# Reordering the start of both halves of a gated MLP stage: store order, adapter factors and a separate buffer for gated rows

## The chip, the cores and the metric

One core of a Trainium2 chip runs the whole program. The metric is the device time in microseconds of one execution; the median of several runs counts. All matrix products are in float32: each operand is split into a rounded part and a remainder, and every product is three matmuls (high x high, high x low, low x high).

## What is computed

Two residual layers on x of 8 x 256 x 1024. The first is a linear layer whose weight is quantised group by group with a codebook of 8 levels and carries a low-rank delta. The second is a gated MLP (gate, up, down, hidden width 2752) with rank-16 adapters picked for each batch row.

```python
# first layer, 1024 x 1024
lora_delta = lora_B @ lora_A * (32.0 / 64)
wg = (weight + lora_delta).reshape(O, I // 128, 128) / scale
w_q = (cb[searchsorted(thresholds, wg)] - wg + wg) * scale
x = x + x @ (w_q + lora_delta).T
# second layer, F = 2752
def lora_add(base, inp, A, B):
    Ab, Bb = A[0][itok], B[0][itok]          # (8, 16, in), (8, out, 16)
    t = einsum('bri,bni->bnr', Ab, inp)
    return base + einsum('bor,bnr->bno', Bb, t) * 0.5
gate = lora_add(x @ W_gate.T, x, A_gate, B_gate)
up   = lora_add(x @ W_up.T,   x, A_up,   B_up)
act  = silu(gate) * up
x = x + lora_add(act @ W_down.T, act, A_down, B_down)
```

## The kernel before

Every engine has its own program, written out by hand, with its order fixed and semaphores between the engines. An engine that waits holds up all that stands behind it in its program; SyncE (SP) and ScalarE (ACT) also issue the DMAs, in program order.

Stage 1, the first layer, ends at about 230 us. x (2048 tokens) is kept in four column blocks c of 512 tokens. `main(i)` on TensorE is one block of 128 output rows times 512 tokens, 24 matmuls, 5.4 us. There are 32; the last six are 26 and 27 (output block 7, c 0 and 1, called LAST0 and LAST1), 28 and 29 (blocks 6 and 7, c = 2), 30 and 31 (c = 3). Two PSUM banks take turns: `main(i)` waits until `out_x1(i - 2)` on ScalarE has copied the bank to a staging buffer (L1980: `pe.wait_ge(s_x1t, i - 1)`); SyncE then stores it with `store_x1(i)` to `XR_d`.

Stage 2, the gate and up products, runs from 230 to about 1173 us. It is a two-level blocked scheme with seven products in place of eight (Strassen's, in the form with few sums). The work is cut into tiles `it` of the hidden width, 11 for each half h of the tokens (it 0 to 10 and 11 to 21), for each tile m = 0 (gate) and m = 1 (up), and for each of these seven products p. The row is mm = 2 it + m, the product number u = 7 mm + p; a product is 12 matmuls, 2.7 us. Tile 0 and tile 11, the first of each half, are the short ones of 96 rows, with the adapter's A rows riding along in the other 32. What each product needs:
- weights: SyncE loads W rows (`load_wn(mm)`), VectorE transposes four blocks L11, L21, L22, L12 (`w_tr`), SyncE stores them for the second half (`store_wt(mm, n)`, n = 0 to 3, to `WT_d`), GpSimd makes the sums S1, S2 (`w_s12`), the difference that overwrites L21 (`w_s3`, L852) and the one that overwrites L12 (`w_s4`, L860). `w_s3(mm)` waits for the store of L21 in the first half: `gp.wait_ge(s_wst[1], 16 * (mm + 1))`. ScalarE rounds the block of product u to `rh` (`hi(u)`, L994), VectorE makes the remainder `rl` (`lo(u)`, L1335). `hi(3)` takes the block that `w_s3(0)` made.
- tokens: once for each half, seven token operands. SyncE loads them to `xr` (`load_raw`, L535; `load_x` in the second half), in the first half VectorE makes four sums (`x_sum`, L1415), ScalarE rounds (`x_hi(h, q)`, L1007), VectorE takes the remainder (`x_lo(h, q)`, L1344). Product q of the first row waits for `x_lo(h, q)`.
- PSUM is emptied by `take(mm, p)` on VectorE (L1360 to L1378) and the copy of bank 1 to `tm` on ScalarE.
- gate and up adapters: the rows of B for a tile are loaded by `load_bn` (ACT), transposed by `b_tr` (VectorE), subtracted by `b_sub`, rounded by `b_hi` (ACT), their remainder made by `b_lo`, and spread by `store_bs(it, g)` (SyncE, six small DMAs, L532) to `bs`. The factors of the tokens are `ts`: `ts_hi` (ACT, L1070) and `ts_lo` (VectorE, L1427), made in the first tile of each half out of `take(row, 2)` and `take(row, 4)`. TensorE first uses them in `ride_lora(h, 0)` before product 8 of the half (L1864).
- the gated rows: `silu` and `gated(it, n)` (L1445) leave four blocks in `ev[:, 1]`. They are stored raw (`store_raw`, ACT), summed by GpSimd (`act_sum(it, 0..3)`, L868 to L879) and stored (`store_s`, SyncE), and multiplied by the down adapter's A on TensorE (`td(n)`, L1893 and L1894) with its own rounding and remainder (`a_hi`, `a_lo`, L1421; `ad` from the transposed rows `ar`, which share the buffer `tm`). `take` of the next up row waits until all this is done.
- W_down is transposed into `dt_` on VectorE and combined on GpSimd in four rounds between rows 13 and 20, the others from row 29 on.

Stage 3, from 1173 us on, multiplies the stored products with W_down.

Of the kernel before, what the change touches and what calls it, by code (L numbers as in the profile page):

```python
# [23 lines left out]
def cond_resid_kernel(  # L24
# [84 lines left out]
    with ctx:  # L109
# [205 lines left out]
        dt_ = aux("dt", [P, 4, CH], f32, 2)  # L315
        araw = aux("araw", [P, 4, DI], f32, 2)
# [157 lines left out]
        with nc.Block() as block:  # L474

            @block.sync
            def _(sp):
# [86 lines left out]
                def dn_load(rd, half):  # L564
                    if rd == 0 and half == 0:
                        sp.wait_ge(s_xts, 64 * XTN)
                    if rd == DN1 and half == 0:
                        sp.wait_ge(s_tdst, 16 * 4)
                    wait(sp, s_dtr, 4 * rd + 2 * half)
# [163 lines left out]
                store_wt(0, 1)  # L733
# [105 lines left out]
            def _(gp):  # L839
# [22 lines left out]
                def act_sum(it, n):  # L862
                    r = slice(0, rows_of(jof(it)))
                    a11, a12, a21, a22 = (ev[r, 1, n_, :] for n_ in range(4))
# [78 lines left out]
                for u in range(END + 7):  # L943
# [10 lines left out]
                    turn = (5, 5, 7, 7) if first(it - 1) else (4, 4, 6, 6) if it == NJ else (1, 1, 3, 4)  # L954
# [29 lines left out]
            def _(act):  # L984
# [69 lines left out]
                def a_hi(n):  # L1054
# [4 lines left out]
                    nc.scalar.copy(ah[r, :], ev[r, 1, (0, 3, 1, 2)[q], :]).then_inc(s_ah, 1)  # L1059
# [23 lines left out]
                def store_raw(it, q):  # L1083
# [3 lines left out]
                    act.dma_start(LT_d[(M1, M4, M2)[q], h, j, r, :], ev[r, 1, (0, 3, 2)[q], :]).then_inc((s_a11, s_a22, s_a21)[q], 16)  # L1087
# [146 lines left out]
                for u in range(END):  # L1234
# [15 lines left out]
                    if (mm, p) == (NM // 2 + 1, 6):  # L1250
# [858 lines left out]
```

## Time and profile before

| | us |
|---|---|
| median of 3 runs (1591.92 to 1593.32) | 1592.16 |
| the profiled execution | 1591.67 |
| its span, first to last instruction | 1590.0 |
| TensorE (PE) busy | 1566.0 (98%) |
| VectorE (DVE) busy | 1236.0 (78%) |
| ScalarE (ACT) busy | 565.9 (36%) |
| GpSimd (POOL) busy | 531.1 (33%) |
| chain that ended last: PE / DVE / issue / DMA | 88% / 6% / 2% / 1% |

TensorE is busy nearly all the time, its mean granted clock is 0.997 of full speed. The share of the span says little about the change; what matters are the few microseconds at which TensorE has nothing to do, who ends them, and what that engine did before. In the rows, "[2.33 <-ACT ts L1070]" behind an instruction is the idle time of its engine just before it and what ended it; "x4" is the number of instructions of one merged piece.

### The profile page before, as it was taken

Reading aid. Unit: us, or ns where it says so; the run is one execution under the profiler, and the core shown is the slowest. Engines: PE = TensorE matmul, PEld = TensorE weight load, DVE = VectorE, ACT = ScalarE, POOL = GpSimd, SP = SyncE. Lnnn points to the kernel's source line nnn. Section 1 sums busy time; section 2 is a strip of 40 time slices with the busy share of each in tenths; the row PEclk is TensorE's granted clock in tenths of the full one; section 3 lists DMA queues with packets and bytes.
Section 4 is the critical chain, followed back from the end, with each engine's and each line's share of the span. In section 5 each row is a group of like instructions: output and inputs, shape, how many; then the busy total and the mean of one; then the engine's idle time right before and its main releaser. Section 6 shows DMA issues by size and latency. Waiting matters only on the chain.

```text
span 1590.0 us, 21056 instructions
## 1 busy us (share of the span) xinstructions
PE 1566.0 (98%) x6936; PEld 1286.9 (81%) x6936; DVE 1236.0 (78%) x1583; ACT 565.9 (36%) x1005; POOL 531.1 (33%) x401
## 2 busy tenths in 40 slices
PE   7999999999999999998999999999999999999999
PEld 5888887888888888886888888888888888888887
DVE  8999869888888999988777887878776576795453
ACT  6311146333333333365333333333343233233231
POOL 4410022465654565625344555556410000000000
PEclk9999999999999999999999999999999999999999
DMA  9652274567777888782435666666468667676553
GB/s 303 133 111 82 68 226 104 149 204 221 222 218 191 224 234 220 232 279 70 122 119 144 185 182 183 162 182 177 141 199 222 157 174 196 160 214 204 159 184 119
DMA packets 368460, 281.25 MB, mean 177 GB/s; under 512 B 225120, under 2 KB 266848, under 8 KB 368224
## 3 DMA queue, kind: packets, MB, share of 16 engines
q1 hardware_dynamic: 246976, 240.77, 52.7%
q10 hardware_dynamic: 119296, 33.33, 9.0%
q0 software_dynamic: 2080, 5.80, 1.9%
q8 instruction: 57, 0.93, 0.2%
q14 instruction: 51, 0.42, 0.1%
HBM read 166.27 MB, written 110.85 MB: 174 GB/s over the span
## 4 chain that ended last, share of the span: by engine, by line
PE 88%; DVE 6%; issue 2%; DMA 1%; ACT 1%; ACTq 1%; SPq 0%; DVEq 0%
PE bank L1842 20%; PE bankA L1842 14%; PE bankC L1842 13%; PE bank L2077 10%; PE bankC L2077 7%; PE bankA L2077 6%; PE bankT L1990 5%; PE bank L1990 5%; PE bankT L2077 3%; DVE xl L1344 1%; PE bankT L1893 1%; PE bankT L1894 1%; PE bankC L1858 1%; DVE rl L1335 1%; DMA xr<-XR_d 1%
## 5 line engine op out<-in xcount | busy, mean ns | idle before, releaser
L994 ACT CAST rh<-wt 128x512 fp32r<-128x512 f32 x253 | 155.2, 620 | 387.8 <-PE bank L1842 92.9
L1335 DVE TENSOR_TENSOR rl<-wt,rh 128x512 fp32r<-128x512 f32 x253 | 241.9, 964 | 35.6 <-ACT rh L994 35.4
L1504 DVE TENSOR_TENSOR opl<-opl,oph 128x512 fp32r<-128x512 f32 (+1 forms) x154 | 107.8, 701 | 155.5 <-ACT oph L1131 155.4
L1842 PE MATMUL bank<-xh,rh 128*128 128x512 f32 x528 | 206.1, 390 | 1.0 <-DVE rl L1335 0.5
L1842 PE MATMUL bank<-xl,rh 128*128 128x512 f32 x528 | 205.7, 390 | 0.0
L1842 PE MATMUL bank<-xh,rl 128*128 128x512 f32 x528 | 205.6, 389 | 0.0
L1131 ACT CAST oph<-opl 128x512 fp32r<-128x512 f32 (+1 forms) x154 | 95.5, 621 | 268.7 <-DMA opl<-LT_d 263.6
L1842 PE MATMUL bankA<-xh,rh 128*128 128x512 f32 x352 | 138.5, 393 | 0.0
L1842 PE MATMUL bankA<-xl,rh 128*128 128x512 f32 x352 | 138.4, 393 | 0.0
L1842 PE MATMUL bankA<-xh,rl 128*128 128x512 f32 x352 | 138.2, 393 | 0.0
L1842 PE MATMUL bankC<-xh,rh 128*128 128x512 f32 x352 | 137.4, 390 | 0.3 <-DVE xl L1344 0.3
L1842 PE MATMUL bankC<-xh,rl 128*128 128x512 f32 x352 | 137.1, 390 | 0.0
L1842 PE MATMUL bankC<-xl,rh 128*128 128x512 f32 x352 | 137.1, 389 | 0.0
L1842 PEld LDWEIGHTS bank<-xh,rh 128*128 128x128 f32 x528 | 99.1, 188 | 23.6 <-issue 1.5
L845 POOL TENSOR_TENSOR wt<-wt 128x512 f32<-128x512 f32 x33 | 46.7, 1416 | 211.8 <-DVE wt L1329 180.2
L1842 PEld LDWEIGHTS bank<-xh,rl 128*128 128x128 f32 x528 | 99.1, 188 | 20.7
L1842 PEld LDWEIGHTS bank<-xl,rh 128*128 128x128 f32 x528 | 99.2, 188 | 20.5
L1360 DVE TENSOR_TENSOR ev<-bankA,tm 128x1024 f32<-128x1024 f32 x44 | 53.5, 1216 | 52.7 <-PE bankA L1858 48.8
L860 POOL TENSOR_TENSOR wt<-wt 128x512 f32<-128x512 f32 x33 | 49.6, 1504 | 121.5 <-DMA WT_d<-wt 85.5
L2077 PE MATMUL bank<-opl,oph 128*128 128x512 f32 (+1 forms) x231 | 90.0, 390 | 0.0
L2077 PE MATMUL bank<-oph,opl 128*128 128x512 f32 (+1 forms) x231 | 90.0, 389 | 0.0
L2077 PE MATMUL bank<-oph 128*128 128x512 f32 (+1 forms) x231 | 89.9, 389 | 0.0
(214 smaller groups left out, 3644.2 us busy)
## 6 DMA issues: line engine op xcount, KB each, us to landing
opl<-LT_d SPq DMA_DIRECT2D x148, 256.0 KB, 2.9
WT_d<-wt SPq DMA_DIRECT2D x88, 256.0 KB, 3.3
RT_d<-dt SPq DMA_DIRECT2D x70, 256.0 KB, 3.2
opl<-RT_d SPq DMA_DIRECT2D x70, 256.0 KB, 3.8
LT_d<-ev ACTq DMA_DIRECT2D x60, 256.0 KB, 2.7
wb<-WT_d SPq DMA_DIRECT2D x44, 256.0 KB, 3.4
wt<-WT_d SPq DMA_DIRECT2D x44, 256.0 KB, 3.5
dn<-in_L_cond_W_down_dram SPq DMA_DIRECT2D x86, 128.0 KB, 3.8
```

The source lines that it names most:

```text
L845: tt(wsrc(mm, S1), wsrc(mm, L21), wsrc(mm, L22), ALU.add).then_inc(s_sum, 1)
L860: tt(wsrc(mm, L12), wsrc(mm, L12), wsrc(mm, S2), ALU.subtract).then_inc(s_sum, 1)
L994: nc.scalar.copy(rh[:, v % RING, 0:KH * rows], wsrc(mm, RSRC[p])).then_inc(s_hi, 1)
L1131: nc.scalar.copy(oph[0:rows, L_AT[n % NL], :], opl[0:rows, L_AT[n % NL], :].bitcast(f32)).then_inc(s_lh, 1)
L1335: dv.tensor_tensor(rl[:, v % RING, 0:KH * rows], wsrc(mm, RSRC[p]), rh[:, v % RING, 0:KH * rows].bitcast(f32), ALU.subtract).then_inc(s_lo, 1)
L1344: dv.tensor_tensor(xl[:, s, k:k + 2, :], xr[:, s, k:k + 2, :], xh[:, s, k:k + 2, :].bitcast(f32), ALU.subtract).then_inc(s_xlo, 1)
L1360: dv.tensor_tensor(e[:, 0:2, :], bankA[r, :, :], tm[r, None, :].to_broadcast([r.stop, 2, CH]), ALU.add).then_inc(s_ev, 1)
L1504: dv.tensor_tensor(opl[0:rows, L_AT[n % NL], :], opl[0:rows, L_AT[n % NL], :].bitcast(f32), oph[0:rows, L_AT[n % NL], :].bitcast(f32), ALU ...
L1842: last = te.matmul(OUT[p], a[:, u % RING, cols], b[:, OPND[p], k, :], start=k == 0 and n == 0, stop=k == KH - 1 and n == 2 and (p in (0, 1 ...
L1858: te.matmul(OUT[p][0:rows, :], bs[:, m, t, half * rows:(half + 1) * rows], ts[:, t, m, :], start=False, stop=True).then_inc(s_pd, 1)
L1990: last = te.matmul(bankY[i % 2], a[o % 3][:, k, :], b[c][:, k, :], start=(k == 0 and n == 0), stop=(k == KD - 1 and n == 2))
L2077: last = te.matmul(out_, a[0:rows, L_AT[n % NL], tok], b[0:rows, R_AT[k], :], start=(k == 0 and i == 0), stop=(k == NJ - 1 and i == 2))
```

## The change

It has three parts.
- The start of stage 2, first half. On SyncE `store_wt(0, 1)`, which stood ahead of the token loads, goes behind the last of them, behind `store_bs(0, 0)`, `store_bs(0, 1)` and `store_wt(0, 3)`; the loads of the up weights of tile 0 (`load_wn(1)`) and the other stores are re-sorted. On ScalarE `load_bn(1)` and `b_hi(1)` come into the last part of stage 1, `out_x1` of block 6, c = 2, ahead of `load_wa(1)`, and `x_hi(0, 3)` ahead of the last `out_x1`. On VectorE `b_tr(1)`, `b_sub(1)`, `b_lo(1)` come ahead of the loop, the four `x_sum` stand together, `w_tr(1, 0)` and `w_tr(1, 1)` go behind `x_lo(0, 2)`.
- The start of the second half. The gated rows of tile 10 go to a buffer of their own, `gx`, in the place of `dt_`, and the transposed adapter rows of tile 11 to `arx`, in the place of `dn`. The waits that protected `ev` in row 23 are gone; in their stead `gated(10, 0)` waits for the W_down stores and the fifth W_down round for all users of `gx`.
- What is done with tile 10's rows moves: `act_sum(10, 0..3)` from products 4, 4, 6, 6 of tile 11 to products 12, 12 and to 2, 3 of tile 12; `a_hi` from 3, 8, 10 to 8, 11, 13, `a_lo` from 5, 9, 10 to 9, 11, 13, `td` from 3, 8, 10, 12 to 3, 10, 12 and 0 of tile 12; `ad_lo(11)`, `td_copy(0)` and `take_td(0)` to products 1 and 2 of tile 12.

```diff
@@ the buffers
+        gx = aux("gx", [P, 4, CH], f32, 2)
+        arx = aux("arx", [P, 2, 2, Q], f32, 1)
+        def gate(it, r, q):
+            return gx[r, q, :] if it == NJ - 1 else ev[r, 1, q, :]
+        def down_rows(it):
+            return arx if it == NJ else ar
@@ SyncE
                 sp.wait_ge(s_main, LAST0 + 1)
-                store_wt(0, 1)
                 load_raw(0, 0, KH, 0, s_x[0])
                 load_raw(1, 0, KH, 3, s_x[3])
...
                 load_raw(1, KH, KD - 1, 6, s_x[6])
+                store_bs(0, 0)
+                store_bs(0, 1)
                 store_wt(0, 3)
-                load_wn(1)
+                store_wt(0, 1)
+                store_x1(TURN[KD - 2, 2])
                 store_wt(0, 0)
                 store_wt(0, 2)
+                load_wn(1)
+                store_x1(TURN[KD - 1, 2])
                 store_bd(KD - 1)
-                store_x1(TURN[KD - 2, 2])
-                store_x1(TURN[KD - 1, 2])
-                store_bs(0, 0)
                 store_x1(TURN[KD - 2, 3])
                 store_x1(TURN[KD - 1, 3])
-                store_bs(0, 1)
@@ sums_at, SyncE
-                    return (6, 7, 8, 9) if first(it - 1) else (5, 6, 7, 8) if it == NJ else (1, 2, 4, 5)
+                    return (6, 7, 8, 9) if first(it - 1) else (13,) if it == NJ else (1, 2, 4, 5)
...
+                    if it == NJ + 1 and 7 * m + p in (0, 3, 4):
+                        store_s(NJ - 1, 1 + (0, 3, 4).index(7 * m + p))
@@ GpSimd
-                    turn = (5, 5, 7, 7) if first(it - 1) else (4, 4, 6, 6) if it == NJ else (1, 1, 3, 4)
+                    turn = (5, 5, 7, 7) if first(it - 1) else (12, 12, None, None) if it == NJ else (1, 1, 3, 4)
...
+                    if u == 14 * (NJ + 1) + 2:
+                        act_sum(NJ - 1, 2)
+                    if u == 14 * (NJ + 1) + 3:
+                        act_sum(NJ - 1, 3)
@@ ScalarE, ahead of the loop
                 hi(3)
                 hi(4)
+                load_bn(1)
+                x_hi(0, 0)
+                out_x1(TURN[KD - 2, 2])
                 load_wa(1)
-                x_hi(0, 0)
                 bd_copy(KD - 1)
-                out_x1(TURN[KD - 2, 2])
                 out_x1(TURN[KD - 1, 2])
+                b_hi(1)
                 x_hi(0, 1)
                 out_x1(TURN[KD - 2, 3])
                 x_hi(0, 2)
+                x_hi(0, 3)
                 out_x1(TURN[KD - 1, 3])
-                x_hi(0, 3)
@@ ScalarE, in the loop
-                    act_tail(u, (6, 8, 10) if first(it - 1) else (3, 8, 10) if it == NJ else (0, 3, 6))
+                    act_tail(u, (6, 8, 10) if first(it - 1) else (8, 11, 13) if it == NJ else (0, 3, 6))
@@ VectorE, take
-                        if m == 1:
+                        if m == 1 and it != NJ:
                             wait(dve, s_a11, 16 * it)
@@ VectorE, gated
+                    if it == NJ - 1 and n == 0:
+                        dve.wait_ge(s_ds, 4 * DN1)
+                        for sem_ in s_raw + s_dst:
+                            dve.wait_ge(sem_, 16 * DN1)
@@ VectorE, ahead of the loop
                 x_sum(0)
                 x_lo(0, 0)
+                b_tr(1)
+                b_sub(1)
                 x_sum(1)
                 x_sum(2)
+                x_sum(3)
+                b_lo(1)
+                x_lo(0, 1)
+                x_lo(0, 2)
                 w_tr(1, 0)
                 w_tr(1, 1)
-                x_lo(0, 1)
-                x_lo(0, 2)
-                x_sum(3)
@@ VectorE, in the loop
-                    dve_tail(u, (6, 8, 10) if first(it - 1) else (5, 9, 10) if it == NJ else (1, 4, 7))
+                    dve_tail(u, (6, 8, 10) if first(it - 1) else (9, 11, 13) if it == NJ else (1, 4, 7))
@@ TensorE
-                    td_at(u, (6, 8, 10, 12) if first(it - 1) else (3, 8, 10, 12) if it == NJ else (0, 3, 6, 9))
+                    td_at(u, (6, 8, 10, 12) if first(it - 1) else (3, 10, 12, None) if it == NJ else (0, 3, 6, 9))
+                    if u == 14 * (NJ + 1):
+                        td(4 * NJ - 1)
```

## Rows read from the trace of the kernel before

**Rows 1.** Busy time by stretch: PE, PEld, DVE, ACT, POOL (instructions), granted clock, DMA share, GB/s

```profile
230.00:260.00 30.00, 26.65 (x107) 20.53 (x106) 28.52 (x32) 17.51 (x28) 8.31 (x6) 0.94 0.39 103
320.00:700.00 380.00, 379.57 (x1673) 313.60 (x1672) 332.35 (x406) 138.62 (x244) 214.64 (x157) 1.00 0.81 224
...
256.66:260.07 3.41, 3.41 (x10) 2.67 (x9) 3.41 (x5) 1.47 (x4) 1.28 (x1) 0.51 0.43 115
```

**Rows 2.** Timeline of TensorE: start us, duration us, engine, line, operation, idle before

```profile
219.00 0.39 PE L1990 MATMUL bank<-lxh,lwh 128*128 128x512 f32 x1
...
256.35 0.52 PE L1864 MATMUL bankC<-ts,bs 128*96 128x512 f32 x1 [2.33 <-ACT ts L1070]
```

**Rows 3.** Timeline of TensorE at the start of the second half

```profile
722.24 0.47 PE L1893 MATMUL bankT<-ah,ad 128*128 128x512 f32 x1 [2.40 <-DVE al L1421]
...
726.68 0.71 PE L1864 MATMUL bankC<-ts,bs 128*96 128x512 f32 x1 [3.52 <-issue]
```

**Rows 4.** Timeline of ScalarE: `hi(3)`, `x_hi(0, 0)`, `out_x1(28)`; four issues of `load_an`

```profile
209.15 0.63 ACT L994 CAST rh<-wt 128x512 fp32r<-128x512 f32 x1
...
210.56 2.00 ACT L1007 CAST xh<-xr 128x1024 fp32r<-128x1024 f32 x2 [0.27 <-issue]
...
217.83 0.58 ACT L1173 COPY x1t_st<-bank 128x512 f32<-128x512 f32 x1
...
716.45 1.89 ACTq L1043 DMA_DIRECT2D an<-Ad_d  x4
```

**Rows 5.** Timeline of GpSimd: `w_s3(0)`

```profile
205.30 1.29 POOL L852 TENSOR_TENSOR wt<-wt 128x512 f32<-128x512 f32 x1
```

**Rows 6.** Line L497 from 202 to 203 us: the store of L21, issued 202.86

```profile
DMA to landing us min/median/max: 2.2/2.2/2.2
```

**Rows 7.** Timeline of SyncE's DMA issues: last token load, first and last of six `store_bs`

```profile
209.72 0.84 SPq L535 DMA_DIRECT2D xr<-XR_d  x1
...
220.18 1.21 SPq L532 DMA_DIRECT2D bs<-bh  x2
...
223.34 0.59 SPq L532 DMA_DIRECT2D bs<-bt  x1
```

**Rows 8.** Line L497 from 216.3 to 216.6 us: a store issued 216.38

```profile
DMA to landing us min/median/max: 8.4/8.4/8.4
```

**Rows 9.** Timeline of VectorE at the first start: `x_sum`, `x_lo`, `take(0, 4)`, `b_tr(1)`

```profile
214.16 2.29 DVE L1415 TENSOR_TENSOR xr<-xr 128x2048 f32<-128x2048 f32 x1 [3.06 <-DMA xr<-XR_d]
...
221.45 5.60 DVE L1415 TENSOR_TENSOR xr<-xr 128x2048 f32<-128x2048 f32 x2 [2.60 <-DMA xr<-XR_d]
...
236.17 4.63 DVE L1344 TENSOR_TENSOR xl<-xr,xh 128x1024 fp32r<-128x1024 f32 x4 [1.19 <-ACT xh L1007]
...
252.58 1.23 DVE L1372 TENSOR_TENSOR ev<-bank,ev 128x1024 f32<-128x1024 f32 x1
...
254.32 0.44 DVE L1385 STREAM_TRANSPOSE bt<-bn 128x256 f32<-128x256 f32 x1
```

**Rows 10.** Timeline of VectorE: `ts_lo` alone, at the second start, beside one GpSimd operation

```profile
273.02 0.88 DVE L1427 SCALAR_TENSOR_TENSOR ts<-ev,half_of,ts 32x256 fp32r<-32x256 f32 x2
...
716.79 2.84 DVE L1427 SCALAR_TENSOR_TENSOR ts<-ev,half_of,ts 32x256 fp32r<-32x256 f32 x2
...
721.40 0.69 DVE L1421 TENSOR_TENSOR al<-ev,ah 128x512 fp32r<-128x512 f32 x1
...
722.37 1.41 DVE L1335 TENSOR_TENSOR rl<-wt,rh 128x512 fp32r<-128x512 f32 x1
723.81 2.77 DVE L1427 SCALAR_TENSOR_TENSOR ts<-ev,half_of,ts 32x256 fp32r<-32x256 f32 x2
...
743.49 1.92 DVE L1427 SCALAR_TENSOR_TENSOR ts<-ev,half_of,ts 32x256 fp32r<-32x256 f32 x2
```

**Rows 11.** Timeline of GpSimd at the second start: `act_sum(10, 3)`, `w_s4(23)`

```profile
723.19 1.71 POOL L879 TENSOR_TENSOR s1a<-ev 128x512 f32<-128x512 f32 x1
724.86 1.44 POOL L860 TENSOR_TENSOR wt<-wt 128x512 f32<-128x512 f32 x1
```

More of the change, by code:

```diff
@@ L863, in act_sum @@
                     r = slice(0, rows_of(jof(it)))
-                    a11, a12, a21, a22 = (ev[r, 1, n_, :] for n_ in range(4))
+                    a11, a12, a21, a22 = (gate(it, r, n_) for n_ in range(4))
                     if n == 0:
@@ L1058, in a_hi @@
                     wait(act, s_tdm, n)
-                    nc.scalar.copy(ah[r, :], ev[r, 1, (0, 3, 1, 2)[q], :]).then_inc(s_ah, 1)
+                    nc.scalar.copy(ah[r, :], gate(it, r, (0, 3, 1, 2)[q])).then_inc(s_ah, 1)
                 def ts_hi(h, m, t):
@@ L1086, in store_raw, with ad_hi @@
                     act.wait_ge(s_av, 3 * it + q + 1)
-                    act.dma_start(LT_d[(M1, M4, M2)[q], h, j, r, :], ev[r, 1, (0, 3, 2)[q], :]).then_inc((s_a11, s_a22, s_a21)[q], 16)
+                    act.dma_start(LT_d[(M1, M4, M2)[q], h, j, r, :], gate(it, r, (0, 3, 2)[q])).then_inc((s_a11, s_a22, s_a21)[q], 16)
+                def ad_hi(it):
+                    act.wait_ge(s_ar, it + 1)
+                    wait(act, s_tdm, 4 * it)
+                    wait(act, s_z, 1)
+                    for t in range(2):
+                        ins = nc.scalar.copy(ad[:, :, t, t, 0, :], down_rows(it)[:, :, t, :])
+                    ins.then_inc(s_adh, 1)
                 def act_tail(u, at_):
@@ L1249, in _ @@
                         a_hi(4 * (it - 1))
[L1250 to L1261 removed]
+                    act_tail(u, (6, 8, 10) if first(it - 1) else (8, 11, 13) if it == NJ else (0, 3, 6))
+                    if (m, p) == ((1, 0) if it % NJ in (0, 1) else (0, 5)) and 0 < it < NIT - 1:
+                        b_hi(it + 1)
+                    if live and m == 1 and p == (5 if it % NJ == 1 else 4) and it != NJ:
+                        ad_hi(it)
+                    if u == 14 * (NJ + 1) + 1:
+                        ad_hi(NJ)
+                        td_copy(0)
                     if (m, p) == ((1, 1) if first(it) else (1, 6)) and it != NJ - 1 and it + 2 < NIT:
@@ L1268, in _ @@
                         wait(act, s_ev, 4 * (mm - 1) + 1)
-                        if m == 0:
+                        if m == 0 and it != NJ + 1:
                             wait(act, s_ad, it)
@@ L1284, in _ @@
                         store_raw(it, p // 2 - 1)
-                    if it < NIT and first(it) and (m, p) == (0, 2):
+                    if it == NJ and (m, p) == (0, 2):
                         load_bn(it + 1)
@@ L1362, in take @@
                     if p == 3:
-                        if m == 1:
+                        if m == 1 and it != NJ:
                             wait(dve, s_a21, 16 * it)
@@ L1368, in take @@
                     if p == 4:
-                        if m == 1:
+                        if m == 1 and it != NJ:
                             wait(dve, s_a22, 16 * it)
@@ L1473, in dn_tr @@
                     wait(dve, s_dst[(0, 1, 3, 2)[b]], 16 * rd)
+                    if rd == DN1 and b == B11:
+                        dve.wait_ge(s_as, 4 * NJ)
+                        dve.wait_ge(s_al, 4 * NJ)
+                        for sem_ in (s_a11, s_a22, s_a21):
+                            dve.wait_ge(sem_, 16 * NJ)
                     if rd == DN1:
@@ L1752, in _ @@
                             dve.wait_ge(s_an, 128 * (it + 1))
-                            dve.wait_ge(s_ev, 4 * mm + 1)
-                            dv.transpose(tm[:, 0:P],
+                            if it == NJ:
+                                dve.wait_ge(s_dtr, 4 * DN1)
+                            else:
+                                dve.wait_ge(s_ev, 4 * mm + 1)
+                            dv.transpose(down_rows(it)[:, :, :, :].rearrange("p f t r -> p (f t r)"),
                                          an[:, :, :, :].rearrange("p f t r -> p (f t r)")).then_inc(s_ar, 1)
-                        if p == 6 and it % NJ != NJ - 1:
+                        if p == 6 and it % NJ != NJ - 1 and it != NJ:
                             ad_lo(it)
+                    if u == 14 * (NJ + 1) + 2:
+                        take_td(0)
+                        ad_lo(NJ)
                     for rd in range(NJ):
@@ L1767, in _ @@
                             dn_tr(rd, B22)
-                    if mm == NM // 2 + 1 and p == 6:
-                        take_td(0)
                     if mm == NM // 2 + 4 and p in (3, 4):
```

22 lines of the change are left out of this document (7 added, 15 removed).

## The prediction

> **What bounds the kernel now.** I read the stretches of the span first, then TensorE's idle gaps, then for each gap the order of time of the engine that ends it. Between 320 and 700 us TensorE is busy 379.57 of 380 us [rows 1]: nothing that leaves its work alone can gain there. What can be won or lost lies in two places. From 230 to 260 us it is busy 26.65 of 30 us, at a mean clock of 0.94 [rows 1]. The longest wait there is for the second adapter matmul of the first row (`ride_lora(0, 0)`), which starts at 256.35 after 2.33 us of idle [rows 2]; the stretch behind it runs 3.41 us at a granted clock of 0.51 [rows 1], the 1.2 GHz level of the two, after the engine had stood still, which is another 3.41 x 0.49 = 1.7 us. The second place is the start of the second half: 2.40 us for the remainder `al` (`td(41)`) and 3.52 us before `ride_lora(1, 0)` at 726.68 [rows 3], again followed by a low clock. In both the reader is to see VectorE working without a pause: it is the engine that comes late. A third point has no gap yet: `main(30)` starts at 219.00 [rows 2] and needs the copy `out_x1(28)`, which ScalarE starts at 217.83 and takes 0.58 us over [rows 4]. That is 0.6 us of slack, and much of the change lies ahead of it.
>
> **Part 1, SyncE's order at the first boundary.** The token rows of half a layer are now asked for ahead of `store_wt(0, 1)`; that saves them one issue (about 0.4 us). What decides is where the store goes: from 202.86 to behind the last token load, behind twelve adapter stores (`store_bs(0, 0)` and `(0, 1)`) and behind `store_wt(0, 3)`. Somebody waits for it: `w_s3(0)` on GpSimd overwrites the block L21 with L11 - L21 and must first see it stored. Now it runs at 205.30 [rows 5], because the store was issued at 202.86 and landed in 2.2 us [rows 6]. Behind `w_s3(0)` stands ScalarE's `hi(3)` (it copies that block), and ScalarE and VectorE work in program order. So in turn:
> - SyncE is through with the last token load at 209.72 + 0.84 = 210.56; six adapter stores take 223.34 + 0.59 - 220.18 = 3.75 us of issue [rows 7], twelve 7.5, one weight store about 0.45: the store of L21 goes out at 218.5 instead of 202.86.
> - Its landing is not to be seen in the trace of before at that time. Bounds: 2.2 us with a quiet queue [rows 6], 8.4 us for the one at 216.38 that had a weight load and others ahead of it [rows 8]. I take 2.5, near the quiet one, since the weight load of tile 1 is now behind the store and the last token load (11.7 us for 0.75 MB while sharing the queue with it) should be done by 217. Landing 221.0, `w_s3(0)` 1.29 us [rows 5], so `hi(3)` at 222.4 instead of 209.15 [rows 4].
> - ScalarE then has `hi(4)`, the four issues of `load_bn(1)` (1.9 us, as four issues of `load_an` [rows 4]), `x_hi(0, 0)` (2.0 us) and the copy of 0.58 us [rows 4]: `out_x1(28)` ends at 222.4 + 0.1 + 1.9 + 2.0 + 0.6 = 227.0. `main(30)` starts there, not at 219.00: TensorE stands 8 us and takes about 1 us more at the low clock. The last x1 product ends at 239.1 (now 229.9) and the first gated stage's product 8 would be reached at 261.1.
> - VectorE: `lo(3)` and `lo(4)` stand behind `hi(3)`, `x_sum(0)` can start 2.0 us after it, at 224.4 instead of 214.16 [rows 9], +10.2. From there its work runs on without its two pauses of 2.60 and 1.19 us [rows 9], which are covered now, -3.8. `b_tr(1)`, `b_sub(1)`, `b_lo(1)` come in front (0.44, 0.29 and 0.38 us, the first in [rows 9]), with two hand-overs: +1.4. The two sums that took 5.60 us [rows 9] beside a GpSimd operation take 2 x 2.29, -1.0. `take(0, 4)`, now at 252.58 [rows 9], ends 6.8 us later. Without `b_tr(1)` between it and `ts_lo(0, 0, 1)` a little is won: `ride_lora(0, 0)` at 263.05 instead of 256.35, **+6.7 us**. TensorE, there at 261.1, still waits 2 us and pays its 1.7 us of low clock as before.
> So here the moved sums (`x_sum(3)` in one go) and the early factors of tile 1 do what they say, save about 3 us of pauses and 1.1 us behind the ride, and are paid for by a start 10 us late. Moved past `load_wn(1)` on SyncE are also `store_x1(28)` and two weight stores; SyncE waits for `out_x1(28)` until 227, so the weights of tile 1 are asked for at 228 to 233. `w_tr(1, 0)` needs them at about 241: hidden. The adapter stores land long before `b_tr(1)` at 229, and its rows too: hidden.
>
> **Part 2, the second half.** Four things leave VectorE's way to `ts_lo(1, 0, 1)`. The remainder `a_lo(41)` moves from ahead of it to product 9: -0.6 us (0.69 busy [rows 10]). GpSimd's four `act_sum(10, ...)` (the last of them, 1.71 us from 723.19, covers most of the second `ts_lo` [rows 11]) go to products 12 and, of the next tile, 2 and 3. `ts_lo` takes 0.88 us when GpSimd is idle, 1.92 beside one operation of it, and 2.84 and 2.77 here [rows 10]. `w_s3(23)` moves up beside the first `ts_lo` and `w_s4(23)`, at 724.86 in [rows 11] and released by `lo(163)`, beside the second, so I take 1.92 for both: -0.9 and -0.85 (bound: -1.9 each if nothing overlaps, 0 if the overlap stays). `lo(163)` drops from 1.41 [rows 10] to 0.69: -0.7. Sum **-3.1 us**: the ride at 723.6. `td(41)` is no longer in front of it and costs nothing where it is now (its two operands are made one and two products earlier). The 2.40 us wait before it does not come back on its own; it only becomes part of the wait for the ride, 719.9 to 723.6. The low clock behind is 1.7 to 2.1 us in either case.
> The Trainium skill's page "SBUF — State Buffer", section "SBUF: two separate sides", says the pair of ports that VectorE and GpSimd share is held for a whole instruction and that the loser blocks fully. By that a `ts_lo` could lose a whole GpSimd operation, some 1.3 to 1.7 us; part 2 would then be -2.3 instead of -3.1.
> The new buffer `gx` adds waits to `gated(10, 0)` for stores of W_down tiles that SyncE issues three products (8 us) earlier at the latest: nothing. `take` of row 23 no longer waits; it didn't wait long before. `td_copy(0)`, `take_td(0)` and `ad_lo(11)` go two or three products later, before `td(44)` needs them: nothing; if that cover failed, some 1.8 us of VectorE time would be late there.
>
> **Sum.** Against the profiled execution, 1591.67 us with a span of 1590.0: +6.7 - 3.1 = +3.6, so 1595.3; the median of the three runs is 0.5 above it, 1592.16, and goes to **1595.8 us**.
>
> **The rivals.**
> - The second boundary gives all back (not slower). If both `ts_lo` fall to 0.88 and the low clock goes too, part 2 is -5.2 - 1.9 = -7.1 and the time 1591.8. For it: the waits there are 5.9 us and VectorE is the only cause. Against: `w_s4(23)` is released just as the second `ts_lo` starts. Chance 0.14.
> - The late store is hidden (faster). If `w_s3(0)` were not in the way, the start would win the two pauses less the wait for the adapter stores, some -3 with the low clock -4.7, and the time would be 1584 to 1587. Against: there is no other path from the store to `hi(3)`. This is also the case that the change does what its order intends. Chance 0.08.
> - The late store is later still (slower). With the 8.4 us of [rows 8], `hi(3)` comes at 228.3 and everything behind it 5.9 later: 1601.7. It decides where the queue is still full at 218.5. Chance 0.1.
> - One of the moved steps crowds its new place (sums beside VectorE at products 12 to 14, `td(42)` at product 12 with its remainder only one product earlier): +1 to +3 on the forecast. Chance 0.08.
> The Trainium skill's page "DMA: Bandwidth & Descriptors", section "Queues, rings and completion order", says that on each DMA engine descriptors are consumed in ring order, which speaks against this change: the store of L21 would have to wait for all that was asked for ahead of it. That is the mechanism of the third rival, whose price stands above from a row.
>
> **How the numbers follow.** The forecast's own case has 0.6 and reaches from 1593 to 1598.5 (landing of 2.2 to 3.8 us, part 2 from -2.3 to -4.5). The range down to 1590.0 takes in the first rival, up to 1600.0 the fourth and the lower part of the third; left out are the hidden store and the full queue. A difference of 0.2%, 3.2 us, is about what a measurement of this kernel tells from none: 1595.4 is its edge, and the forecast lies just beyond. Of its 0.6 I put 0.36 beyond and 0.24 within; with the rivals: slower 0.36 + 0.10 + 0.07, same 0.24 + 0.14 + 0.01, faster 0.08.
>
> **What would show it.** Right: `w_s3(0)` (L852 of before) near 221, the rh casts 3 and 4 near 222.5, a TensorE gap of about 8 us in the x1 products at 219, the first `xr` sum on VectorE near 224.4, the ride at 263. In the second half, `ts_lo` of 1.8 to 2 us and one gap of 3 to 4 us instead of two. Wrong: no gap at 219, or the weight store landing by 212; then the whole first term falls. If `ts_lo` keeps 2.8 us without `act_sum` beside it, part 2 shrinks to -1.3.

## The result, and the profile after

| | before | after |
|---|---|---|
| median of 18 runs each, us | 1591.96 | 1596.34 |
| lowest to highest, us | 1587.91 to 1594.29 | 1593.06 to 1598.59 |
| profiled execution, us | 1591.67 | 1595.51 |
| its span, us | 1590.0 | 1593.9 |

The change makes the kernel slower: the ratio is 1.0025, 95% interval 1.0019 to 1.0032, or 4.4 us by the medians. The forecast was 1595.8 us, with a range of 1590 to 1600.

One thing first, for every comparison of traces below. The part of the program ahead of the change isn't equally long in each execution: the last transpose, just ahead of `main(28)`, comes 0.72 us later in after than in before, and 0.65 to 2.24 us later in ten of the eleven other traces that were taken, 0.36 us earlier in one. "Net" below means that this start is taken off.

TensorE after the change, in the same view as [rows 1]: from, to, length, busy time of PE, PEld, DVE, ACT and POOL, granted clock, DMA share, GB/s:

```profile
219.00:228.00 9.00, 1.02 (x5) 0.52 (x4) 3.87 (x3) 3.80 (x7) 2.95 (x3) 0.79 0.35 101
228.00:231.00 3.00, 3.00 (x7) 2.35 (x8) 2.97 (x4) 0.47 (x1) 0.00 (x0) 0.50 0.85 295
230.00:260.00 30.00, 30.00 (x131) 24.74 (x131) 29.66 (x29) 17.14 (x23) 6.89 (x5) 0.98 0.33 101
...
264.31:268.00 3.69, 3.69 (x16) 3.10 (x17) 3.37 (x4) 2.20 (x5) 1.30 (x1) 1.00 0.50 133
326.00:706.00 380.00, 379.61 (x1673) 313.46 (x1672) 332.42 (x406) 139.40 (x244) 214.51 (x157) 1.00 0.80 224
```

TensorE stands still from 219.9 to 227.87, where it had no gap [rows 2], and starts again at half clock, the 1.2 GHz level. The middle is untouched: 0.4 us idle in 380, as in [rows 1]. And there is a surprise in the fourth line: behind the wait for the first ride the granted clock is 1.00, where it was 0.51 in before.

The chain of the first gap, in the timelines of SyncE (the last adapter store and two weight stores, the second of which is the store of L21), GpSimd, ScalarE and VectorE of after:

```profile
218.52 0.59 SPq L542 DMA_DIRECT2D bs<-bt  x1
219.16 1.06 SPq L507 DMA_DIRECT2D WT_d<-wt  x2
```

```profile
222.18 1.26 POOL L865 TENSOR_TENSOR wt<-wt 128x512 f32<-128x512 f32 x1 [16.07 <-DMA WT_d<-wt]
223.38 0.53 POOL L955 MEMSET ad<- 128x512 f32 x1
223.87 1.26 POOL L873 TENSOR_TENSOR wt<-wt 128x512 f32<-128x512 f32 x1
```

```profile
223.48 0.62 ACT L1011 CAST rh<-wt 128x512 fp32r<-128x512 f32 x1 [13.49 <-POOL wt L865]
...
227.24 0.58 ACT L1198 COPY x1t_st<-bank 128x512 f32<-128x512 f32 x1
```

```profile
224.13 2.15 DVE L1358 TENSOR_TENSOR rl<-wt,rh 128x512 fp32r<-128x512 f32 x2 [15.77 <-ACT rh L1011]
226.20 2.28 DVE L1438 TENSOR_TENSOR xr<-xr 128x2048 f32<-128x2048 f32 x1
228.51 2.36 DVE L1367 TENSOR_TENSOR xl<-xr,xh 128x1024 fp32r<-128x1024 f32 x2
230.79 0.44 DVE L1408 STREAM_TRANSPOSE bt<-bn 128x256 f32<-128x256 f32 x1
...
263.33 0.88 DVE L1450 SCALAR_TENSOR_TENSOR ts<-ev,half_of,ts 32x256 fp32r<-32x256 f32 x2
```

The reader is to see one wait handed on three times. GpSimd stood 16.07 us for the store, ScalarE 13.49 us for GpSimd's `w_s3(0)`, VectorE 15.77 us for ScalarE's cast. TensorE, with a gap of 7.98 us, then gets `out_x1(28)`:

```profile
227.87 0.79 PE L2029 MATMUL bank<-lxh,lwh 128*128 128x512 f32 x1 [7.98 <-ACT x1t_st L1198]
...
264.31 0.44 PE L1903 MATMUL bankC<-ts,bs 128*96 128x512 f32 x1 [1.82 <-ACT ts L1087]
...
729.48 0.71 PE L1903 MATMUL bankC<-ts,bs 128*96 128x512 f32 x1 [3.34 <-issue]
...
743.71 0.47 PE L1932 MATMUL bankT<-ah,ad 128*128 128x512 f32 x1 [0.39 <-DVE al L1444]
```

The last two rows are the second half. Its two waits of 2.40 and 3.52 us [rows 3] are one of 3.34 us, and there is a new small one at `td(42)`. VectorE and GpSimd there:

```profile
722.87 1.80 DVE L1450 SCALAR_TENSOR_TENSOR ts<-ev,half_of,ts 32x256 fp32r<-32x256 f32 x2
...
726.80 0.65 DVE L1358 TENSOR_TENSOR rl<-wt,rh 128x512 fp32r<-128x512 f32 x1
727.48 1.89 DVE L1450 SCALAR_TENSOR_TENSOR ts<-ev,half_of,ts 32x256 fp32r<-32x256 f32 x2
...
742.87 0.69 DVE L1444 TENSOR_TENSOR al<-gx,ah 128x512 fp32r<-128x512 f32 x1
```

```profile
722.24 1.75 POOL L865 TENSOR_TENSOR wt<-wt 128x512 f32<-128x512 f32 x1
727.58 1.51 POOL L873 TENSOR_TENSOR wt<-wt 128x512 f32<-128x512 f32 x1 [3.60 <-DVE rl L1358]
```

The account of the 3.8 us between the two profiled executions, by how far the same instruction is shifted: start +0.72; first ride +7.96, so +7.24 for the change; +6.36 a few products behind it (-1.60, the low clock that did not come) and +6.05 through the middle; +3.61 at the last stage, so -2.44 for the second half; +3.84 at the end.

### The profile page after: what moved, and what is told of

Read it like the earlier page. It is cut to its first block, busy times and chain, and to the rows that moved or that the text cites. A ratio compares the mean times of both kernels' runs of the same rounds, so it can differ in the third digit from the quotient of the medians.

```text
span 1593.9 us, 21059 instructions
## 1 busy us (share of the span) xinstructions
PE 1565.2 (98%) x6936; PEld 1286.7 (81%) x6936; DVE 1240.1 (78%) x1583; ACT 566.3 (36%) x1005; POOL 528.7 (33%) x401
## 4 chain that ended last, share of the span: by engine, by line
PE 87%; DVE 7%; issue 3%; ACT 1%; DMA 1%; ACTq 1%; SPq 0%; POOL 0%; DVEq 0%; POOLq 0%
PE bank L1881 19%; PE bankA L1881 14%; PE bankC L1881 13%; PE bank L2118 10%; PE bankC L2118 7%; PE bankA L2118 6%; PE bank L2029 4%; PE bankT L2029 4%; PE bankT L2118 3%; DVE xl L1367 2%; PE bankT L1932 1%; PE bankT L1933 1%; PE bankC L1897 1%; DVE rl L1358 1%; PE bankA L1897 1%
## 5 line engine op out<-in xcount | busy, mean ns | idle before, releaser
L873 POOL TENSOR_TENSOR wt<-wt 128x512 f32<-128x512 f32 x33 | 47.4, 1437 | 108.7 <-DMA WT_d<-wt 71.1
```

The source lines that it names most:

```text
L873: tt(wsrc(mm, L12), wsrc(mm, L12), wsrc(mm, S2), ALU.subtract).then_inc(s_sum, 1)
```

## The experiments

Theory A, from the trace: the late store of L21 is the whole loss, and without it the first part would win what its other edits save. Rival: something else of the first part costs too. The first four runs take the change apart.

**One statement back.** The kernel after, with the store of L21 ahead of the token loads as in before:

```diff
                 sp.wait_ge(s_main, LAST0 + 1)
+                store_wt(0, 1)
                 load_raw(0, 0, KH, 0, s_x[0])
...
                 store_wt(0, 3)
-                store_wt(0, 1)
```

> The changed kernel with one line put back: the store of block L21 of tile 0 goes out ahead of the token loads again, all else stays. Theory (the late store holds up hi(3), and through it out_x1(28), main(30), x_sum(0)): no TensorE gap in the x1 products at 219, w_s3(0) back at 205 to 206, x_sum(0) near 214, ride_lora(0, 0) at 252 to 255, time 10 to 12 us below the changed kernel, 1584 to 1587. Rival 1 (the early adapter factors make a new wait of the same size: b_tr(1) on VectorE behind the twelve adapter stores): x_sum(1) starts at 222 or later, ride not before 256, time 1588 to 1591. Rival 2 (the gap at 219 comes from something else): gap stays, time 1595 or more.

Measured: 1591.27 us (11 runs), ratio to before 0.9999 (0.999 to 1.0008). 5.1 us of after come back by moving one store, and the gap at 219 is gone. But it is 1591, not 1584 to 1587: the number of rival 1, at the upper edge of its range. The timeline of VectorE in this kernel says why:

```profile
213.84 2.29 DVE L1438 TENSOR_TENSOR xr<-xr 128x2048 f32<-128x2048 f32 x1 [1.34 <-DMA xr<-XR_d]
216.16 2.36 DVE L1367 TENSOR_TENSOR xl<-xr,xh 128x1024 fp32r<-128x1024 f32 x2
225.44 0.45 DVE L1408 STREAM_TRANSPOSE bt<-bn 128x256 f32<-128x256 f32 x1 [6.92 <-DMA bs<-bt]
...
227.10 6.89 DVE L1438 TENSOR_TENSOR xr<-xr 128x2048 f32<-128x2048 f32 x3
```

`b_tr(1)` overwrites `bt` and must see the adapter stores landed. SyncE issued the last of them at 219.10, and they took up to 6.2 us to land (line L542, issues of 218.5 and 219.1):

```profile
DMA to landing us min/median/max: 4.7/5.5/6.2
```

So VectorE stands 6.92 us with three token sums behind the waiting instruction, and TensorE gets a new wait in the first gated products, with a low clock behind it (a mean of 0.64 from 236.70 to 241.00):

```profile
236.70 0.47 PE L1881 MATMUL bankA<-xh,rh 128*128 128x512 f32 x1 [2.54 <-issue]
```

In after this wait is invisible, since VectorE reaches `b_tr(1)` only at 230.79: the late store hid it.

**The first part alone**, on the kernel before (all edits of the first boundary, none of the second half; this diff stands for them):

```diff
+                store_bs(0, 0)
+                store_bs(0, 1)
                 store_wt(0, 3)
-                load_wn(1)
+                store_wt(0, 1)
...
                 x_lo(0, 0)
+                b_tr(1)
+                b_sub(1)
                 x_sum(1)
                 x_sum(2)
+                x_sum(3)
```

> The kernel before with only the first-half part (orders of SyncE, ScalarE, VectorE ahead of the loop). Theory: an 8 us gap ahead of main(30), ride_lora(0, 0) 6.5 to 7.5 us late, one low-clock stretch of 1.7 us possibly gone: 1597 to 1599. Rival (both parts are needed together, they interact): not within 1 us of the sum before + 6.5.

Measured: 1599.77 us (4 runs), ratio 1.0052 (1.0036 to 1.0068): +7.8 us, 0.8 above the upper edge of what was expected. The ride's net shift is +8.1, more than the 7.2 of after. The difference is on ScalarE, in the eight DMA issues (`load_an`) ahead of its casts: from the first to the end of the last they took 5.20 us here (two of 1.91 us together, then six of 3.26) and 3.66 us in after, and VectorE's remainders waited 0.68 us for the casts.

```profile
259.06 3.26 ACTq L1043 DMA_DIRECT2D an<-Ad_d  x6
262.42 1.14 ACT L994 CAST rh<-wt 128x512 fp32r<-128x512 f32 x2 [3.48 <-issue]
```

**SyncE's order alone.** Before, with only the list of SyncE's issues at the first boundary taken from after, and VectorE's and ScalarE's orders left alone.

> The kernel before with only SyncE's new order ahead of the loop; ScalarE and VectorE as before. Theory: the same late store, hi(3) at 222 to 223, a gap of about 8 us ahead of main(30), and as w_tr(1, 0) stands ahead of the token remainders and its weights are asked for late, 2 to 3 us more on VectorE: ride_lora(0, 0) 9 to 11 us late, 1600 to 1602. Rival (the gap needs load_bn(1) and x_hi(0, 0) ahead of out_x1(28)): gap under 3 us, time under 1596.

Measured: 1601.83 us (one run), its span 1600.2. The same chain: `w_s3(0)` at 222.42 after 16.14 us of waiting, a gap of 8.15 us. The net shift of the ride is +8.5. The highest of 15 runs of before beside it was 1593.73 us, so one run is enough to see the loss. So the order of SyncE is the loss, and the other edits of the first part win back 0.4 us of it at the ride, by one trace of each.

**The second part alone**, on the kernel before (`act_sum(10, ...)`, `a_lo(41)`, the new `gx`, the later `td` steps):

```diff
-                    turn = ... else (4, 4, 6, 6) if it == NJ else ...
+                    turn = ... else (12, 12, None, None) if it == NJ else ...
...
-                    td_at(u, ... else (3, 8, 10, 12) if it == NJ ...)
+                    td_at(u, ... else (3, 10, 12, None) if it == NJ ...)
```

> The kernel before with only the second-half part of the change (gx, arx, moved sums, a_hi, a_lo, td). Theory: the two waits of 5.9 us there become one of 3.5, of the 3.1 us won about 0.6 are lost again at td(42): 2.4 us below the kernel before, 1589 to 1590. Rival (what was won in the changed kernel at this point came from the first part's disturbance): 0 to 1 us below.

Measured: 1587.56 us (6 runs), ratio 0.9976 (0.9963 to 0.999). It beats both kernels, and is 1.4 us below the expected range. In its trace the second half wins only 1.2 us (shift -2.53 in the middle, -3.77 at the last stage), with 5.12 us at a clock of 0.50 behind the ride. The rest, 3.6 us net of the start, came ahead of it, in code that is the same in both kernels. 1.6 of that is one event: no low clock behind the first ride. The other 2.0 are shorter waits (none of 0.48 us at 238.68, one of 0.31 us and not 0.28 and 0.81 us at the down adapter's matmuls near 306 and 319) and shifts that I can't assign. That ride has the same wait as in [rows 2], 2.33 us, but the stretch behind it has a granted clock of 1.00 and not of 0.51 [rows 1]:

```profile
257.01 0.44 PE L1898 MATMUL bankC<-ts,bs 128*96 128x512 f32 x1 [2.33 <-ACT ts L1087]
```

```profile
257.50:261.00 3.50, 3.50 (x17) 2.89 (x16) 3.50 (x6) 1.92 (x4) 1.30 (x1) 1.00 0.44 114
```

By the medians the parts are +7.8 and -4.4 us, +3.4 together, and the whole change is +4.4. With intervals of about 2.5 and 2 us to either side of the parts, an interaction between them is not shown.

**The wait in store_back taken away.** Theory B: what is left in `store_back` is the 6.92 us in front of `b_tr(1)`.

```diff
                 x_lo(0, 0)
-                b_tr(1)
-                b_sub(1)
                 x_sum(1)
                 x_sum(2)
                 x_sum(3)
-                b_lo(1)
                 x_lo(0, 1)
                 x_lo(0, 2)
+                b_tr(1)
+                b_sub(1)
+                b_lo(1)
```

> This is the kernel of the run store_back (the change with the L21 store ahead of the token loads again), with the factors of tile 1 (b_tr(1), b_sub(1), b_hi(1), b_lo(1)) moved from ahead of the three later token sums to behind x_lo(0, 2). Theory: in store_back VectorE stood 6.92 us in front of b_tr(1), for the twelve adapter stores that SyncE issues behind the last token load, and all three sums stood behind it; that made the 2.54 us wait of TensorE at 236.70 and the low clock behind it. With b_tr(1) behind the sums x_sum(1) starts near 221, as in the kernel before, TensorE has no wait near 236, and the first adapter matmul pair comes 1 to 4 us earlier than in store_back: 1586 to 1589 us. Rival (the remaining cost is the landing of the token rows, or the sums in one go): x_sum(1) does not start before 224, and the time stays within 1 us of store_back, 1590.5 to 1592.

Measured: 1587.18 us (8 runs), ratio 0.9966 (0.9954 to 0.9978). `x_sum(1)` comes 2.49 us after the operation ahead of it and not behind a wait of 6.92, and of the gap in the first gated products 0.69 us is left:

```profile
218.55 2.36 DVE L1367 TENSOR_TENSOR xl<-xr,xh 128x1024 fp32r<-128x1024 f32 x2
223.41 8.00 DVE L1438 TENSOR_TENSOR xr<-xr 128x2048 f32<-128x2048 f32 x3 [2.49 <-DMA xr<-XR_d]
```

Theory B holds: 4.1 us below `store_back`, 9.2 below after. Yet it is level with the second part alone (1587.56), so the first part, freed of both waits, gives less than can be measured here: the pause for the token rows stays (2.49 us; 2.60 in [rows 9]), and the net shift of the ride is -0.1. The profiled execution was the slowest of the eight, 1592.12 us: it has the low clock behind both rides, and four of the others had a mean granted clock of 1.000.

**Why `ts_lo` takes 1.9 us.** The second part alone, with `w_s4(23)` held until the second `ts_lo` is done:

```diff
+                        if mm == NM // 2 + 1:
+                            gp.wait_ge(s_tlo, 6)
                         w_s4(mm)
```

> This is the kernel before with the second-half part alone, and w_s4(23) on GpSimd held back until the second ts_lo of the second half is done. It tells why that ts_lo takes 1.89 us. Theory (VectorE and GpSimd slow each other while both work): the second ts_lo takes 0.88 to 0.95 us, the ride comes 0.9 to 1.0 us earlier after the take ahead of it, and the time is 1586 to 1587 us, against 1587.6 for that part without the hold. Rival (the ts_lo is slow there for a cause of its own, or w_s4 is late for the product after): ts_lo stays near 1.9 us, or a new wait of 0.5 to 1 us appears for the weight remainder, and the time is 1587.5 to 1588.5.

Measured: 1587.61 us (10 runs), ratio 0.9973 (0.9962 to 0.9984).

```profile
719.99 0.88 DVE L1450 SCALAR_TENSOR_TENSOR ts<-ev,half_of,ts 32x256 fp32r<-32x256 f32 x2
...
721.35 2.16 DVE L1358 TENSOR_TENSOR rl<-wt,rh 128x512 fp32r<-128x512 f32 x2 [0.15 <-ACT rh L1013]
...
725.50 1.78 DVE L1444 TENSOR_TENSOR al<-gx,ah 128x512 fp32r<-128x512 f32 x1
```

The same pair of instructions takes 0.88 us with GpSimd idle and 1.89 beside its one operation: the overlap is the cause. The excess of the ride's gap falls from 3.49 to 2.66 us (excess: how much later a matmul starts than 0.23 us behind the one before it, the usual distance here). But the time does not move. The overlap has only changed its victim: the two weight remainders behind the `ts_lo` now run beside the held-up `w_s4(23)` and take 2.16 us. In the second part alone they are these 1.29 us:

```profile
721.11 1.29 DVE L1356 TENSOR_TENSOR rl<-wt,rh 128x512 fp32r<-128x512 f32 x2
```

So the remainder for `td(41)`, behind them, comes no earlier (it takes 1.78 us here and 1.77 there, beside GpSimd in both), and TensorE, which now comes earlier, waits for it (0.68 us of excess).

**The crowding of td(42), a missed shot.**

```diff
-                    act_tail(u, ... (8, 11, 13) if it == NJ ...)
+                    act_tail(u, ... (7, 11, 13) if it == NJ ...)
...
-                    dve_tail(u, ... (9, 11, 13) if it == NJ ...)
+                    dve_tail(u, ... (8, 11, 13) if it == NJ ...)
```

> This is the kernel before with the second-half part alone, and the two operands of td(42) (ah on ScalarE, al on VectorE) made one product earlier, at products 7 and 8 and not 8 and 9. Theory: the 0.56 us excess of TensorE in front of td(42) is the crowding of that step, so it goes, and the time is 0.5 us below the 1587.6 us of that part, 1586.8 to 1587.3. Rival: al one product earlier pushes the ts_lo behind it (0.88 us) into the next GpSimd operation or the take behind it, and 0.3 to 1 us is lost there: 1587.5 to 1588.5.

Measured: 1588.64 us (10 runs), ratio 0.9977 (0.9968 to 0.9987), the excess at `td(42)` still 0.56 us. The expectation names the wrong step: the first entry of these lists belongs to `td(41)`. The run moved operands that were not late, gained nothing, and says nothing on `td(42)`.

**Moving what waits.** If VectorE is late at one point only, work that is moved behind this point on TensorE should not wait. The first run moves the pair of the ride by a product. The second also moves the pair behind it and `td(41)`, and makes the remainder for `td(42)` ahead of the `ts_lo` beside it. The third makes the second's edits on the kernel of `store_back_b_late`.

```diff
-        RIDE = {8: 0, 14: 1}
+        RIDE = {9: 0, 14: 1}
-        LATE = {10: 0, 16: 1}
+        LATE = {11: 0, 16: 1}    # second and third run
```

> This is the kernel before with the second-half part alone, and the first pair of adapter matmuls of each half (ride_lora(0, 0) and (1, 0)) with the take that needs them moved from ahead of product 8 to ahead of product 9, 5.4 us later on TensorE. Theory: the two waits (2.49 and 3.5 us) are only VectorE's lateness at that one point, and VectorE has 2.65 to 3.4 us of idle right behind them, so both waits go, and with them the low clock behind (1.7 and 2.4 us where it shows): 1577 to 1582 us. Rival: the lateness is not absorbed; the weight remainders of the ring or the late_lora pair at product 10 come late in their place, half or more of the waits returns there: 1583 to 1587.

Measured: 1589.46 us (10 runs), ratio 0.9987 (0.9974 to 0.9999). One product is 2.72 us, not the 5.4 that the expectation gives. The ride no longer waits. The pair behind it does, for the `take` that moved with the ride, and `td(41)` waits for its remainder:

```profile
262.49 0.70 PE L1898 MATMUL bankC<-ts,bs 128*96 128x512 f32 x2 [1.88 <-DVE ev L1399]
...
727.33 0.47 PE L1927 MATMUL bankT<-ah,ad 128*128 128x512 f32 x1 [2.11 <-DVE al L1442]
```

> The kernel before with the second-half part alone (1587.6 us), and the work that waits for VectorE at the start of each half put later on TensorE: the first adapter pair (ride_lora(h, 0)) and the take behind it from product 8 to 9, the pair after it (late_lora(h, 0)) and its addition from product 10 to 11; a product is 12 matmuls, 2.72 us. td(41) goes from product 10 to 11, and the remainder for td(42) is made ahead of the ts_lo beside it, not behind it. In p2_ride9, where only the first pair was moved, the wait came back as 2.04 us at the late pair and 2.27 us at td(41). Theory: VectorE is behind by a fixed 2 to 3.5 us in each of these stretches and catches up in its idle of 2.65 to 3.4 us behind them, so one product more of room absorbs it. What is left is 0.7 and 1.0 us for the remainder of product 8, and the 0.55 us of td(42) goes: 1582 to 1585 us. Rival: VectorE is the bound over a longer stretch, and a remainder of the weight ring or the addition for product 12 comes late instead; 1 to 2 us of wait stays in each half: 1586 to 1588.

Measured: 1592.05 us (10 runs), ratio 0.9999 (0.9989 to 1.0008), 4.5 us worse than the part it is built on. The wait stands one step further on and is longer, for the addition that must be done before product 12:

```profile
271.09 0.47 PE L1878 MATMUL bankC<-xh,rh 128*128 128x512 f32 x1 [2.70 <-issue]
```

> The same four edits on the kernel of store_back_b_late (the whole change, with the L21 store ahead of the token loads again and the factors of tile 1 behind the sums; 1587.2 us). Theory: as in p2_late11, and the first half as good as or up to 1 us better than there, since b_tr(1) no longer stands between the take and the second ts_lo: 1581 to 1584.5 us. Rival (the first half has no more to give): equal to p2_late11 within 0.5 us.

Measured: 1590.2 us (10 runs), ratio 0.9995 (0.9984 to 1.0006), with the same waits (2.86 us of excess in the first half, 1.70 and 1.59 in the second). In mechanism the rival won three times: VectorE is behind over the whole stretch (28.52 of 30 us busy in [rows 1]), and each step moved on TensorE meets it again. The times, though, lie above the rival's ranges in the first two runs, and the third is 1.9 us off the second, where 0.5 was said. Why the first two lost more than the rival gave them was not looked into further.

**Less in front of the ride.** So the ride's operand has to come earlier on the engine that makes it. On the kernel of `store_back_b_late`, what is not needed for the ride goes behind it in VectorE's and ScalarE's orders (in short, by the names of the steps):

```diff
   VectorE:  - lo(9); ts_lo(0, 0, 1)              + ts_lo(0, 0, 1); lo(9)
             - b_tr(12); lo(163); ts_lo(1, 0, 1)  + ts_lo(1, 0, 1); lo(163); b_tr(12)
             - ts_lo(1, 1, 0); a_lo(42)           + a_lo(42); ts_lo(1, 1, 0)
   ScalarE:  - hi(9); ts_hi(0, 0, 1)              + ts_hi(0, 0, 1); hi(9)
             - hi(163); ts_hi(1, 0, 1)            + ts_hi(1, 0, 1); hi(163)
```

The operands of `td(41)` are again made one product earlier.

> The kernel of store_back_b_late (1587.2 us) with less in front of the second adapter factor of each half on both engines: on VectorE the weight remainder lo(9) (and lo(163)) goes behind ts_lo(h, 0, 1), and b_tr(12) behind it too; on ScalarE the cast hi(9) (and hi(163)) goes behind ts_hi(h, 0, 1); the remainder for td(42) is made ahead of the ts_lo beside it, and the operands of td(41) one product earlier. Since lo(163) releases GpSimd's w_s4(23), that operation too comes behind the ts_lo. Theory (the wait for the ride is the sum of the operations of VectorE ahead of it, 0.65 for a remainder, 0.44 for b_tr, 1.0 for the overlap with GpSimd, and the 0.55 to 0.6 of the cast on ScalarE): the first ride comes 0.6 us earlier, the second 1.4 to 2.0, td(42) has no wait, and the time is 1582 to 1585 us. Rival (as with the pairs moved later: what is moved away is late at its new place): waits of the same size appear at products 8 to 10 for lo(9), lo(163) or al, and the time stays at 1586.5 to 1588.

Measured: 1584.87 us (5 runs), ratio 0.996 (0.9946 to 0.9973): the best of all, 6.4 us below before in the same set and 11.5 below after. The interval still overlaps that of `store_back_b_late`; that it beats that one is probable, not shown. Both rides, and the second `ts_lo` of the second half:

```profile
257.45 0.44 PE L1909 MATMUL bankC<-ts,bs 128*96 128x512 f32 x1 [1.74 <-ACT ts L1087]
...
720.67 0.44 PE L1909 MATMUL bankC<-ts,bs 128*96 128x512 f32 x1 [1.74 <-ACT ts L1087]
```

```profile
719.68 0.88 DVE L1452 SCALAR_TENSOR_TENSOR ts<-ev,half_of,ts 32x256 fp32r<-32x256 f32 x2 [0.31 <-ACT ts L1087]
```

```profile
721.20:725.00 3.80, 3.80 (x18) 3.17 (x17) 3.68 (x6) 3.00 (x7) 1.30 (x2) 1.00 0.05 8
```

The second ride waits 1.74 us instead of 3.34, with no low clock behind it, `td(42)` has no wait, and in front of both rides the last step is now ScalarE's `ts_hi`: VectorE waits for it (0.37 and 0.31 us). GpSimd's operations now slow `b_sub(12)` and `b_lo(12)` (1.18 and 1.52 us, 0.29 and 0.42 in the second part alone), for which the ride does not wait. Some came back here too: the pair at product 10 has 1.22 us of excess.

## Why the prediction was right, point by point

**The late store, the term that decided: right, by its steps.** Forecast and trace of after, the trace with its 0.72 us of later start: store issued 218.5 (about 219.7, the second of the two); landed 2.5 us later (2.3 to 2.6 for the two); `hi(3)` at 222.4 (223.48); `out_x1(28)` done at 227.0 (227.82); a gap of 8 us (7.98 idle) and 1 us at the low clock (1.5); ride +6.7 (+7.24 net). SyncE alone in the new order costs more than that, and one statement moved back takes it away: this cause is shown, not argued. Three terms were too small. The twelve adapter stores took 8.2 us of issue and not 7.5. `lo(3)` and `lo(4)` took 2.15 us, since GpSimd's `w_s4(0)` (L873), which stands behind `w_s3(0)`, now runs beside them. The low clock at 228 took half a microsecond more, but the ride goes by VectorE.

**"TensorE, there at 261.1, still waits 2 us and pays its 1.7 us of low clock as before": half wrong.** The wait was there (1.82 us), the low clock was not, and after was spared 1.60 us. A stand of 2.33 us had a low clock behind it in before and none in the second part alone; 1.82 and 1.95 us had none (after, `store_back`), 2.01, 2.40 and 2.80 us had one (`store_back_b_late`, `sp_order_alone`, `p1_alone`). That of 2.01 us, with a granted clock of 0.50:

```profile
259.64:263.05 3.41, 3.41 (x9) 2.65 (x9) 3.35 (x5) 0.64 (x2) 1.72 (x1) 0.50 0.47 159
```

The sum should have carried this term with both values. That it was right within 1 us owes something to luck: ride +0.5, clock -1.6, start +0.7 and second half +0.7 nearly cancel.

**The second half, forecast -3.1: the ride was right, the stage was not.** The durations came as taken: `ts_lo` 1.80 and 1.89 (1.92 each), the remainder 0.65 (0.69), `a_lo` out of the way. The four sum to 1.04 + 0.88 + 0.76 + 0.60 = 3.28 us, and the ride's shift goes from 6.05 to 2.80, -3.25. But the time won at the end is 2.44. Mis-sized was "`td(41)` costs nothing where it is now": its two matmuls and those behind them are no longer ahead of the ride but behind it, which is 0.45 us of work that only changed place. And rival four's crowding came, at 0.55 us and inside the main case: al for `td(42)` is made behind a `ts_lo` and ends at 743.56, some 0.4 us after TensorE is free for it. A low clock shorter by 0.48 us gave some of it back; 0.3 us are small shifts that I can't assign.

**The rivals.** The second boundary did not give all back: both `ts_lo` stayed at 1.8 to 1.9, as the row of `w_s4(23)` said [rows 11], and `p2_hold` shows why for the second. "The late store is hidden, 1584 to 1587" was priced wrongly: with the store out of the way the time is 1591.3, because `b_tr(1)` waits for the adapter stores. The rival names this wait and takes some 0.8 us off for it (pauses of 3.8 us, "some -3"); the prediction calls it hidden where it goes through the main case. Hidden was true of after, where VectorE comes to it at 230.79, and false of the rival's own case, where it comes at 218.5 and stands 6.92 us. A cover that another loss provides goes when that loss is mended. The store later still (8.4 us of landing) did not come: 2.3 to 2.6.

**The two rules that the prediction set against its rows.** The Trainium skill's page "SBUF — State Buffer", section "SBUF: two separate sides", has the loser of the shared ports blocked for the whole of the winner's instruction. The prediction priced this at a whole GpSimd operation more for each `ts_lo`, -2.3 for the second half. The trace agrees with the rule, and not with this price. The `ts_lo` of 1.89 us in after is two instructions (shortest, median and longest in ns, then the first and last start):

```profile
L1450 DVE SCALAR_TENSOR_TENSOR ts<-ev,half_of,ts x2: 480/982/1483, 727.5 to 727.9; 32x256 fp32r<-32x256 f32 x2
```

The first, of 0.48 us, is as short as with GpSimd idle. The second, of 1.48 us, starts at 727.89 with GpSimd's operation (727.58 to 729.09) under way, and ends at 729.37, 0.28 us behind it. All six slowed `ts_lo` instructions at the second start of before and after end 0.28 us behind a GpSimd operation. So what an instruction loses is the rest of the operation that it meets, 1.0 us in this case, and not the whole of 1.51. That -2.3 is near the -2.44 measured is chance: the durations and the ride's -3.25 came as the rows had them.

The Trainium skill's page "DMA: Bandwidth & Descriptors", section "Queues, rings and completion order", has descriptors taken in the order of the ring. No run here shows the order within the ring; that much was still queued ahead of the L21 store at 219.7 is not to be seen in its 2.3 to 2.6 us.

## What to carry to other kernels

When a queue's order is changed for one reader, list every buffer that the moved stores release, and follow each in program order through all engines: here a store that nobody read for long held an engine, and through it three more, for 8 us. Price a rival in its own schedule and not in that of the forecast, since a wait that is covered by your main loss comes out when the loss is gone. And where an engine is behind over a whole stretch, moving the work that waits for it may only move the wait (three runs, no gain); what may pay is to put the awaited operation ahead of others on that engine (2.3 us by the medians, with intervals that still overlap).

## What the runs showed of the hardware that I had not expected

- **The clock behind a short stand is not settled by its length.** 2.33 us of standing was followed by 3.4 us at a granted clock of 0.51 in one kernel and by 1.00 in another, with the same instructions around it. Executions of one kernel differ likewise: six of the second part alone had a mean granted clock of 0.998, 0.999 and 1.000 twice each, with medians of 1589.7, 1587.6 and 1585.6 us. 29 executions of before had 0.996 to 0.998, never more; the five of `ride_first` had 0.999 and 1.000. So a wait taken away may be worth more than its length, by what the clock does behind it. Behind the rides, the shortest stand with a low clock was 2.01 us and the longest without one 2.50 us (the second ride of `p2_hold`); all eight of 3.33 to 3.52 us had one. What decides it in between stays open.
- **A DMA issue on ScalarE can cost twice its usual 0.45 to 0.47 us.** The first two of eight took 0.79 us together in after and 1.91 us in `p1_alone`, and the casts behind them moved the ride. What decides which of the two an execution gets was not tried.
- **The overlap of VectorE and GpSimd moves on.** Kept off `ts_lo` (1.89 to 0.88 us), it came back on the two weight remainders behind it (1.29 to 2.16 us), for no change in the time. In `ride_first` it fell on `b_sub` and `b_lo`, for which no ride waits.
